# The last normalisation of the second gated feed-forward, moved from the vector engine to the scalar engine

## What is computed

```python
def _layer(x, wqkv, qs, ksc, wo, lg, lb, w1, b1, w2, b2):
    ...
    x = x + o @ wo                                  # attention of the block
    h = shift_token(x)
    mu = h.mean(-1, keepdims=True)
    var = h.var(-1, keepdims=True)
    h = (h - mu) / jnp.sqrt(var + 1e-05) * lg + lb
    h = h @ w1 + b1
    a, g = jnp.split(h, 2, axis=-1)
    h = a * jax.nn.gelu(g, approximate=False)
    x = x + h @ w2 + b2
    return x
...
x = _layernorm(x + _L0_ffn_ref(x, ...))             # two _layer calls, then the outer sum and norm
```

## Time and profile before

| what | value |
|---|---|
| time, median of 3 runs | 1542.22 us (1541.38 to 1543.84) |
| profiled execution: time | 1531.8 us |
| its span from first to last instruction | 1530.0 us |
| PE / DVE / ACT / POOL busy | 1246.4 / 1068.6 / 750.6 / 881.5 us |
| busy share of the span | 81% / 70% / 49% / 58% |
| stretch of F1_GLU's sums and norms | about 579 to 646 us |

### The profile page before, as it was taken

The page is one execution under the profiler, slowest core; times in us unless marked ns, Lnnn a source line. Parts: engine busy times, 40 slices in busy tenths (PEclk is TensorE's granted clock), DMA queues, the critical chain, the costliest instruction groups (busy, mean ns, idle before and its releaser), DMA issues.

```text
span 1530.0 us, 38481 instructions
## 1 busy us (share of the span) xinstructions
PE 1246.4 (81%) x13889; PEld 864.4 (56%) x13889; DVE 1068.6 (70%) x2494; ACT 750.6 (49%) x1609; POOL 881.5 (58%) x1114
## 2 busy tenths in 40 slices
PE   7988878887879868689997898774999894899771
PEld 5656645556746557456665565672666663566540
DVE  6876858994679957578885575434777744887874
ACT  3554435554545544244554464343566642556555
POOL 3643448993379955456664563574566633466654
PEclk9999979997989989799999998796999977999995
DMA  9400000000000000000000000115000012000000
GB/s 352 132 1 1 0 0 1 0 0 24 0 1 0 0 1 14 6 2 1 0 0 1 1 0 28 32 46 183 1 1 1 1 37 64 1 0 2 0 0 28
DMA packets 32468, 36.81 MB, mean 24 GB/s; under 512 B 4451, under 2 KB 29283, under 8 KB 31626
## 3 DMA queue, kind: packets, MB, share of 16 engines
q1 hardware_dynamic: 30410, 32.14, 6.3%
q0 software_dynamic: 1984, 3.67, 0.9%
HBM read 26.63 MB, written 9.18 MB: 23 GB/s over the span
## 4 chain that ended last, share of the span: by engine, by line
PE 41%; DVE 20%; POOL 16%; issue 13%; ACT 6%; DMA 3%; POOLq 1%; DVEq 0%; SPq 0%; ACTq 0%
PE ps L345 34%; DVE maxima L442 4%; PE ps L465 4%; POOL arena L538 3%; DVE arena L444 3%; POOL inv_norm L919 3%; POOL arena L924 2%; ACT arena L452 2%; PE ps L839 2%; POOL rstd L383 1%; DVE sq_sum L1058 1%; DMA moe_back<-arena 1%; ACT arena L1249 1%; ACT arena L1015 1%; DVE gate L1825 1%
## 5 line engine op out<-in xcount | busy, mean ns | idle before, releaser
L345 PE MATMUL ps<-arena 64*64 64x64 f32 (+5 forms) x7921 | 399.6, 274 | 25.6 <-ACT arena L459 8.5
L345 PEld LDWEIGHTS ps<-arena 64*64 64x64 f32 (+3 forms) x7921 | 266.1, 143 | 157.7 <-issue 131.9
L538 POOL TENSOR_TENSOR arena<-arena,w_const 128x1024 f32<-128x1024 f32 x96 | 182.3, 1901 | 138.3 <-DVE arena L759 65.8
L442 DVE TENSOR_REDUCE maxima<-ps 128x16 f32<-128x1024 f32 (+1 forms) x144 | 159.1, 1105 | 100.1 <-PE ps L345 100.1
L452 ACT ACTIVATE arena<-arena 128x1024 f32<-128x1024 f32 (+1 forms) x144 | 138.5, 962 | 114.3 <-DVE arena L444 114.0
L444 DVE TENSOR_TENSOR arena<-ps,maxima 128x1024 f32<-128x1024 f32 (+1 forms) x144 | 159.3, 1106 | 4.9
L465 PE MATMUL ps<-w_const,arena 128*128 128x128 f32 x1024 | 141.3, 279 | 21.6 <-ACT arena L452 10.9
L383 POOL TENSOR_TENSOR rstd<-var_eps,minus_half 128x1 f32<-128x1 f32 x144 | 80.5, 570 | 123.6 <-DVE var_eps L888 83.3
L919 POOL TENSOR_TENSOR inv_norm<-sq_floor,minus_half 128x16 f32<-128x16 f32 x32 | 121.9, 3810 | 38.6 <-DVE sq_floor L1061 38.3
L459 ACT COPY arena<-ps 128x1024 f32<-128x1024 f32 (+1 forms) x144 | 131.2, 911 | 23.1 <-PE ps L465 22.7
L465 PEld LDWEIGHTS ps<-w_const,arena 128*128 128x128 f32 x1024 | 114.6, 143 | 35.8 <-ACT arena L452 20.8
(11 more groups left out here) (323 smaller groups left out, 2564.4 us busy)
## 6 DMA issues: line engine op xcount, KB each, us to landing
experts<-in_pack_moe SPq DMA_DIRECT2D x2, 4628.0 KB, 21.2
moe_back<-shT SPq DMA_DIRECT2D x4, 1024.0 KB, 19.4
w_fa<-in_pack_fa SPq DMA_DIRECT2D x2, 1024.0 KB, 11.6
moe_in<-state SPq DMA_DIRECT2D x2, 1024.0 KB, 5.3
arena<-moe_back SPq DMA_DIRECT2D x8, 256.0 KB, 5.0
arena<-moe_back SPq DMA_DIRECT2D x4, 512.0 KB, 5.2
w_a<-in_pack_a SPq DMA_DIRECT2D x1, 1856.0 KB, 17.0
w_fg<-in_pack_fg SPq DMA_DIRECT2D x2, 537.0 KB, 12.1
```

What stands on the lines that cost most here:

```text
L345: return nc.tensor.matmul(o, lhsT, rhs, start=start, stop=stop, skip_group_check=True)
L442: nc.vector.reduce_max(mx, sc, X_AXIS).then_inc(signal["max_ready"], 1)
L538: nc.gpsimd.tensor_tensor(keys_wide(s).rearrange("p (b h t) -> p b h t", b=SEQS, h=8), key8(s).rearrange("p (b t) -> p b t", b=SEQS).unsqu ...
```

## The change

The outer norm of F1_GLU leaves DVE. POOL makes `ln_bias` behind `rstd`, waiting alone for its own `rstd`; ACT does the norm at the end of its step; `norm_tile` goes from DVE's step. Since ACT now reads `total[s]`, DVE's outer sum waits by `wait_last` until the norm of the tile two before is done. The table of semaphores counts `ln_bias` for F1_GLU too.

```diff
-    ... "ln_bias": NARROW + (L0_CROSS, L1_ATTN), ...
+    ... "ln_bias": NARROW + (L0_CROSS, F1_GLU, L1_ATTN), ...
@@ glu_pool, step
                     if ph == F1_GLU:
                         for t, s in tile(4):
                             norm_pool(t, s)
+                            t.wait("ln_rstd", s, alone=True)
+                            nc.gpsimd.tensor_scalar(ln_bias[s][:, :], moments[s][:, 0:1], rstd[s][:, 0:1], -1.0,
+                                                    ALU.mult, ALU.mult).then_inc(signal["ln_bias"], 1)
@@ glu_scalar
+                def norm(t, s):
+                    t.wait("ln_bias", s)
+                    nc.scalar.activation(tile_of(state, t, s), total[s][:, :], ACT.Identity,
+                                         bias=ln_bias[s][:, 0:1], scale=rstd[s][:, 0:1]).then_inc(tile_done, 1)
+
@@ glu_scalar, step, behind gelu
+                    if ph == F1_GLU:
+                        for t, s in tile(4):
+                            norm(t, s)
@@ glu_vector, add
                     else:
+                        t.wait_last(s)
                         nc.vector.tensor_tensor(total[s][:, :], glu_resid(s), bank(s, 3, 0, P), ALU.add)\
                             .then_inc(signal["res_sum"], 1)
@@ glu_vector, step
                     for t, s in tile(0):
                         h_statistics(t, s)
-                    if ph == F1_GLU:
-                        for t, s in tile(4):
-                            norm_tile(t, s)
                     for t, s in tile(3):
                         add(t, s)
```

More of the change, by code:

```diff
@@ L84 @@
     "y_ready": tuple(p for p in FINISHED if p != L3_CROSS),
-    "resid_ready": NARROW + GLU + (L0_CROSS,), "ln_bias": NARROW + (L0_CROSS, L1_ATTN), "sums_ready": WIDE + (L0_CROSS,), "gate_exp": (L0_CROSS,), "gate_den": (L0_CROSS,), "gate_ready": (L0_CROSS,),
+    "resid_ready": NARROW + GLU + (L0_CROSS,), "ln_bias": NARROW + (L0_CROSS, F1_GLU, L1_ATTN), "sums_ready": WIDE + (L0_CROSS,), "gate_exp": (L0_CROSS,), "gate_den": (L0_CROSS,), "gate_ready": (L0_CROSS,),
     "paths_diff": (L0_CROSS,), "diff_gated": (L0_CROSS,),
```

## The result

The changed kernel takes 1547.22 us, the kernel before 1539.72 us in the runs beside it (medians of 16 runs each). The ratio is 1.0045, with a 95% interval of 1.0034 to 1.0056: 0.45% or 6.9 us slower, where 7.0 us were forecast. (The two medians are 7.5 us apart; the ratio with its interval is the better measure.) The 1549.2 us of the forecast were counted from the median of three runs, 1542.22, which lies 2.5 us above that of the sixteen; hence the 2 us between it and 1547.22.

A forecast was written before the change was run, and what follows sets the result against it. The prediction took a ring of waits through POOL and DVE in F1_GLU to bound the kernel. Loop 6.6 us plus drain 0.43, together 7.0, added to 1542.22 gave 1549.2 us, 0.46% slower; range 1544.5 to 1552.5.

The forecast's parts named there:

- The ring: Waits closing each F1_GLU turn: POOL's queue from L383 to L1479, 2.40 us, then DVE back to L383, 1.17; 3.57 us.
- (1): Taking the norm L893, 16 x 0.42 us, from DVE gives 0; upper end 0.42 us a turn.
- (2): POOL's new ln_bias behind L383 lengthens a turn of F1_GLU's loop by 0.43 us.
- (3): POOL's loop branch, now behind the short ln_bias, makes turns with a branch 0.72 us longer in place of 0.43.
- (4): In the drain after the loop, only tile 15's ln_bias lies on the path, costing 0.43 us.
- (5): ACT's norm runs in ACT's idle time before its copy, with 0.6 us to spare: 0.
- (6): DVE's outer sum newly waits for the norm of two tiles before, with 3 us to spare: 0.
- DVE as the pace: Rival: removing L893 from DVE gives 0.42 us in each of twelve turns, 5.0 us faster, 1537.2 us; 4%.
- ACT's norm late: Rival: ACT's norm holds the copies into shT, 0.3 us in each of twelve turns, 3.6 us more, 1552.8; 6%.
- The clock within the loop: Rival: PE's clock falls for two turns, each over 1.4 us more for its up-projections, 1552.0 us; 5%.
- L893 holding POOL up: Rival: removing L893 gives POOL 0.4 us a turn and cancels ln_bias, 1542 to 1544 us; within the no-change case, 7%.

The follow-up runs named there:

- e2: Changed kernel without POOL's ln_bias, ACT's norm taking the tile's mean as bias; ratio 0.9984 to the kernel before, loop 39.41 us.
- e1: Kernel before plus POOL's ln_bias and its lone wait, norm left on DVE; ratio 1.0051 to the kernel before, loop 45.46 us.
- e6: Changed kernel with POOL's residual in F1_GLU moved behind h_rstd; ratio 0.9993 to the kernel before, loop 38.22 us.
- e4: Changed kernel with POOL's ln_bias instruction issued twice, the first into a spare column; ratio 1.0037 to the kernel before, loop 46.68 us.
- e8: Changed kernel itself, run again; ratio 1.0044 to the kernel before, loop 45.00 us.
- e9: Changed kernel with ACT's norm in front of the Gelus instead of behind them; one run, no ratio, loop 45.03 us.
- e3: Changed kernel with ln_bias made by DVE instead of POOL, in front of the outer sum; ratio 1.0005 to the kernel before, loop 39.40 us.
- e5: Kernel before with POOL's residual in F1_GLU moved behind h_rstd; ratio 0.9996 to the kernel before, loop 38.77 us.

## Why the prediction was right, and where its sizes were off

**The ring** was the right one. Three experiments agree: without POOL's bias the spacing is back (e2), with it alone the cost is there (e1), and with the ring shortened elsewhere the same bias costs nothing (e6).

**(1) L893 gives 0**: 0.03 us over the loop in e2. The number is right, one sentence behind it isn't: the sum could not start sooner without L893, because PE's down-projections hold it. For the same reason DVE's idle time in front of the inner norm came to 0.7 or 0.8 us and not to the 1 us of the forecast; another 0.35 to 0.41 us stands in front of the sum.

**(2) `ln_bias`, 0.43 us a turn**: measured 4.04 - 3.60 = 0.44, and L1356 at the forecast 0.95 us behind L383.

**(3) The branch, 0.72 us a turn**: measured 4.18 - 3.57 = 0.61. The mechanism is right (e4) and the size isn't. I took the 0.52 us from L383 to L1356 as the sequencer's time for the branch, but that was how long L383 itself ran; the sequencer needs 0.44 once nothing longer covers it. Two paths that end together show only the longer one, and I read the other off it. So L1356 starts 0.08 us earlier than forecast; another 0.03 us is DVE's own branch, which in the kernel before held the inner norm 0.07 us behind L1346 where it is 0.03 or 0.04 now. Five turns x 0.11 us, 0.6 us too much.

**(4) The drain.** From the twelfth L383 to the thirteenth the change adds 3.72 - 3.39 = 0.33 us, where I had 0.43 for the exit of the loop. So the loop with its exit cost 5.66 + 0.33 = 6.0 us against 6.6 forecast. The `ln_bias` of tile 15 cost more than forecast (POOL's timeline, answering to the earlier trace rows):

```profile
652.21 0.55 POOL L383 TENSOR_TENSOR rstd<-var_eps,minus_half 128x1 f32<-128x1 f32 x1 [2.76 <-DVE var_eps L888]
653.24 0.27 POOL L1373 TENSOR_SCALAR ln_bias<-moments,rstd 128x1 f32<-128x1 f32 x1 [0.48 <-POOL rstd L383]
653.44 0.29 POOL L363 COPY xs<-state 128x128 f32<-128x128 f32 x1
```

The staging copy stands 1.23 us behind L383 and stood 0.50 behind it: 0.73 us, not 0.43, because POOL sat idle for 0.48 us in place of 0.17. That 0.48 is there in e1, e6, e8 and e9 too and not in e4. What it is stays open.

PE's clock moved the drain both ways, as allowed for. The four projections of L1_ATTN's tile 0 fell into the full clock, those of tile 1 further into the lower one. The granted clock was 0.50 from 630 to 632 us before and is 1.00 from 634 to 640 now; for tile 1 it was 0.92 from 650 to 652 and is 0.50 from 652 to 658. Before, then changed:

```profile
629.99 3.60 PE L345 MATMUL ps<-w_a,xT 128*128 128x512 f32 x4 [0.35 <-ACT shT L1231]
...
649.65 2.23 PE L345 MATMUL ps<-w_a,xT 128*128 128x512 f32 x4
```
```profile
638.31 1.98 PE L345 MATMUL ps<-w_a,xT 128*128 128x512 f32 x4 [0.35 <-ACT shT L1231]
...
657.09 3.12 PE L345 MATMUL ps<-w_a,xT 128*128 128x512 f32 x4
```

That is -1.62 and +0.89 us. From the first L383 to the L869 of L1_ATTN's tile 1 the two profiles differ by (660.25 - 583.12) - (651.92 - 580.70) = 5.9 us, in e8's profile by 6.2. The terms above give the same: 6.0 for the loop with its exit, 0.73 for tile 15, and the clock's -1.62 and +0.89. That a sum of 7.0 met a measured 6.9 so closely is partly luck: its ring part was 0.6 too high, the phase itself grew by 5.9 to 6.2, no row here locates the rest, and the interval of the ratio spans 5.2 to 8.6 us.

**(5), (6) ACT's norm and the sum's wait, 0**: shown by e2, and e9 for the wait.

**The rivals.** DVE as the pace: refuted by e1, with which e2 agrees. ACT's norm late: refuted; even in e3, where it ends at the copy, neither the copy nor the ring moves. The clock within the loop: 1.00 throughout. L893 holding POOL up: in the kernel before it costs the ring nothing, but I dismissed it too widely, below.

## What to carry to other kernels

An instruction costs by its place, not its engine's load: find the ring of waits that closes in one turn, and ask of each moved instruction whether it stands in it. POOL waited for 1.2 of every 3.57 us in front of L383 and DVE only for 0.2 to 0.3 in front of the inner norm, and yet 0.26 us on POOL cost 0.44 to 0.6 while 0.42 us taken from DVE gained nothing. Look for the second ring too: it may be level with the first, and then only additions show. Work that the next turn doesn't need belongs in the engine's idle time, in front of the wait that ends it, and what a loop's body ends on decides whether its branch is seen: L383's 0.55 us hid POOL's, `ln_bias` with its 0.26 us didn't. If two engines end together, the releaser that a view names is a guess; move one of them to know.

## What the runs showed of the hardware

Instructions of DVE and POOL that meet within about 0.1 us of their starts can hold each other up, in either direction. L893 takes 0.33 to 0.36 us where it isn't held. In e1 it is held twice in the loop, 0.63 and 0.64 us, when L1359 starts 0.1 us behind it, and it then ends 0.10 us behind L1359. In four other turns with nearly the same starts it is L1359 that takes 0.55 or 0.56 in place of 0.45; and in e5 L1346 takes 0.64 in place of 0.55.

In the loop of the kernel before L893 takes 0.42 to 0.44 us in eleven turns. It starts there during the end of L1359, and 0.05 to 0.07 us before the copy L363. Which of the two holds it was not tested, but in e1 it also starts during the end of an instruction of POOL as large, L1356, and isn't held:

```profile
604.35 0.46 POOL L1356 TENSOR_TENSOR gate<-inner,outT 128x128 f32<-128x128 f32 x1 [0.17 <-issue]
...
604.67 0.35 DVE L893 TENSOR_SCALAR state<-total,moments,rstd 128x128 f32 x1
```

And in the kernel before it ends 0.08 us behind L363 (607.71 against 607.63), much as it ends behind L1359 in e1. That speaks for the copy. I had read from the copy, which keeps its 0.29 us beside L893, that there was no such contention; the cost was in DVE's duration, which I took as the instruction's own.

The Trainium skill, "SBUF — State Buffer", section "SBUF: two separate sides", has the port pair that DVE and GpSimd share held for a whole instruction by the one that starts first, with the other blocked. Whether L893 uses that pair, no row shows; the runs agree that one of the two waits. They differ from it in the rest: in e1 L893 starts first by the records and is still the one held twice, and where L1359 is held it ends at 601.17, where waiting for L893's end at 600.87 and then taking 0.45 us would make it 601.32.

A wait of POOL for its own result costs 0.17 us beyond the result (L1373 behind L383). A hardware loop's branch with its register operations takes POOL's sequencer 0.44 us, from 612.52 to 612.96 in the changed kernel, and DVE's 0.49, from 602.02 to 602.51 in e6.
